# Gated delta-rule attention with mixture of experts on one core: block inverse by joining, decay exponents from spread rows, third value tap on VectorE

## Chip, cores and metric

One core of a Trainium2 chip. The metric is the device time of one launch in microseconds. Everything is fp32.

## What is computed

The reference, cut to the part that matters here (b=2 sequences, t=2048 tokens, 16 heads of 64; a mixture of 64 experts follows in the same launch and is not touched by the change):

```python
q, k, v = (causal_dwconv(x @ W.T, w, bias) for ...)      # 4 taps per channel
g = log_sigmoid(x @ Wg.T); beta = sigmoid(x @ Wb.T)
k = k / clip(norm(k), 1e-12); q = q * Kd ** -0.5
def step(S, inp):                                        # over time, per head
    Sk = einsum('bhkv,bhk->bhv', S, k_t)
    delta = einsum('bhv,bhk->bhkv', v_t, k_t) - einsum('bhv,bhk->bhkv', Sk, k_t)
    S = exp(g_t) * S + b_t * delta
    o_t = einsum('bhkv,bhk->bhv', S, q_t)
x = layernorm(x + o @ Wo.T)
x = layernorm(x + moe(x))
```

## The kernel before, in words

A first phase (`gates_phase`, some 54 us) computes the gates. Their running sums lie with 64 positions on the partitions in `za`; transposed by TensorE they are stored in DRAM as `g_rows`.

The second phase (`delta_phase`, L190) is a software pipeline over 64 macros. A macro `m` is 256 tokens of both sequences for one pair of heads; a chunk is 64 tokens. Slot `t` works on macro `t` (projections, first taps), `t-1` (other taps, gates, masked products), `t-5` (assembling the inverse of a 64x64 triangular matrix per chunk from its 16x16 diagonal blocks) and, from `t-7` on, on the sequential chain over chunks (two chain steps per slot, called one and two). Two macros are a group; the inverses of the 16x16 diagonal blocks are made for a whole group at once, spread over an odd slot and the even slot behind it. Each engine has its own instruction order written out by hand in a loop over the slots (TensorE L534, VectorE L669, ScalarE L811, GpSimd L906, SyncE's DMA queue L345), and semaphores tie them together. What the change touches:

- The convolution has four taps. ScalarE makes tap 3 (`last_tap`, L731) and copies the projection to `hist` (L729); VectorE adds taps 2, 1, 0 for k and q in place (`conv`, L575, line 586). For v it adds taps 2 and 1 (`conv_values`, L589, line 599), and tap 0 is a second product with a diagonal matrix, accumulated in PSUM while TensorE transposes the values (`turn_values`, L403, line 416). The diagonal lies in the last 64 columns of the weight buffer.
- The decay exponents of a macro (key's running sum subtracted from query's, minus infinity above the diagonal) are one product of two operands `arg_l` and `arg_r` (`exponents`, L421), into the single PSUM bank `p_j` that the three projections use too. One ScalarE instruction takes their exponential into `ex` (`decay`, L739, line 744), GpSimd multiplies by beta over the squared key length (`weight`, L886, line 890), VectorE multiplies the products by it (`mask`, L622, line 628).
- The diagonal blocks: 128 partitions hold one 16x16 block each. GpSimd sets `xi` to the identity (L922); `substitute` (L631) then takes 15 rows, each an outer product into `outer` (line 639) and a subtraction from `xi` (line 642), every instruction waiting for the one before it. Row `r` has (15-r)(r+1) elements: 15, 28, 39, 48, 55, 60, 63, 64 and down again. Rows 0 to 7 stand in the odd slot, rows 8 to 14 in the even one.
- `horner` (line 649) subtracts a product in PSUM from the loaded inverse three times per macro, with a product of TensorE between each two (`inverse_ry1`, `inverse_ry2`, line 448). In TensorE's order the third projection, `inverse_ry1`, `products` (L432, line 439) and `inverse_ry2` end a slot. `mask` waits for `products`.
- `lengths` (line 616) sums the squared keys, GpSimd's `clip` (line 877) bounds them, VectorE takes the reciprocal (`inverse_lengths`, line 620), GpSimd makes two factors (883, 884), `weight`, and the square root (`roots`, L893, line 896), by which ScalarE scales the values one slot later (line 792).
- GpSimd also decays the state before each chain step (`decay_state`, line 902), takes out the off-diagonal part (`off_diagonal`, line 872), and copies three columns of history (858, 865).

## Time and profile before

| | us |
|---|---|
| median of 3 runs | 1730.0 (1725.58 to 1736.51) |
| the profiled execution | 1728.8 |
| its span, first to last instruction | 1727.0 |
| busy in the span: TensorE | 1546.2 (90%) |
| VectorE | 1238.0 (72%) |
| ScalarE | 888.3 (51%) |
| GpSimd | 852.2 (49%) |

The span holds three stages: gates up to about 54 us, the delta phase to about 1177 us, the mixer and experts to the end. The shares are means over all of them, so each stage has to be read by itself. PE and PEld are TensorE's products and its weight loads, DVE is VectorE, ACT ScalarE, POOL GpSimd, SP SyncE. A line number L is that of the kernel before. On VectorE, records of neighbours overlap by some 80 ns where the second waits for nothing.

### The profile page before, as it was taken

The numbers are of one execution on the slowest core, as the hardware profiler recorded it, in microseconds if no ns is written. First come the engines' busy times: TensorE is split into PE (matmuls) and PEld (weight loads), VectorE is DVE, ScalarE is ACT, GpSimd is POOL, SyncE is SP. The second block draws the span as 40 slices with busy tenths as digits, with TensorE's granted clock in tenths as the row PEclk, the third lists the DMA queues.
The fourth block names the chain that finished last, engine by engine and source line by source line (L and its number), as shares of the span: only waits on it lengthen the run. The fifth ranks groups of instructions, "written<-read, shape, count | busy, mean of one in ns | idle before, by whom it ended". The sixth has DMA issues, their size and how long they took to land. (4 is left out here: it accounts for less than half of the span.)

```text
span 1727.0 us, 73955 instructions
## 1 busy us (share of the span) xinstructions
PE 1546.2 (90%) x31244; PEld 1160.5 (67%) x31244; DVE 1238.0 (72%) x3061; ACT 888.3 (51%) x2282; POOL 852.2 (49%) x1070
## 2 busy tenths in 40 slices
PE   6678999999999999999999999778899998898980
PEld 6235666666666666666666666666899998887870
DVE  1488999999999999999999999633566665222225
ACT  1466767777777677677777676510111111332333
POOL 0034354344444444435435444312777777677775
PEclk9899999999999999999999999989999999999995
DMA  8345555656556655655665655536565631799658
GB/s 320 87 88 116 126 117 130 133 110 134 129 116 132 126 122 119 141 122 116 128 137 117 126 120 117 114 74 191 175 185 164 186 98 41 208 249 248 135 86 301
DMA packets 521402, 245.45 MB, mean 142 GB/s; under 512 B 423888, under 2 KB 485968, under 8 KB 520176
## 3 DMA queue, kind: packets, MB, share of 16 engines
q1 hardware_dynamic: 367824, 200.45, 44.1%
q10 hardware_dynamic: 134784, 21.25, 7.7%
q0 software_dynamic: 18464, 19.03, 6.3%
q8 instruction: 247, 4.05, 1.0%
q14 instruction: 83, 0.68, 0.1%
HBM read 169.29 MB, written 71.37 MB: 139 GB/s over the span
## 5 line engine op out<-in xcount | busy, mean ns | idle before, releaser
L387 PE MATMUL delta_p_j<-xt,w 128*128 128x512 f32 x768 | 386.1, 626 | 20.6 <-ACT delta_yv L736 8.3
L586 DVE SCALAR_TENSOR_TENSOR delta_kq<-delta_hist,cw,delta_kq 128x512 f32<-128x512 f32 x384 | 315.5, 822 | 22.9 <-ACT delta_kq L736 13.9
L729 ACT ACTIVATE delta_hist<-delta_p_j 128x512 f32<-128x512 f32 x192 | 115.0, 599 | 256.3 <-PE delta_p_j L387 244.3
L902 POOL TENSOR_TENSOR delta_sd<-state,eg_end 128x256 f32<-128x256 f32 x128 | 92.2, 720 | 290.6 <-DVE state L665 290.6
L387 PEld LDWEIGHTS delta_p_j<-xt,w 128*128 128x128 f32 x768 | 131.5, 191 | 135.8 <-issue 101.9
L1406 POOL DMA_INDIRECT slot_tokens<-tokens,mix_slot x192 | 189.3, 986 | 64.0 <-issue 52.2
L877 POOL TENSOR_SCALAR delta_n<-delta_n 128x8 f32<-128x8 f32 x64 | 15.5, 242 | 318.9 <-DVE delta_n L616 318.9
L1176 PE MATMUL mix_p_h<-wo,w 128*88 128x128 f32 x1024 | 127.9, 279 | 13.2 <-ACT wo L1362 12.6
L1176 PEld LDWEIGHTS mix_p_h<-wo,w 128*88 128x88 f32 x1024 | 117.1, 159 | 30.6 <-ACT wo L1362 28.5
L1312 DVE SCALAR_TENSOR_TENSOR wo<-wo,mix_p_h 88x256 f32<-88x256 f32 x64 | 26.7, 417 | 154.7 <-ACT wo L1368 154.7
L792 ACT ACTIVATE delta_kpv<-delta_kpv,delta_root 128x64 f32<-128x64 f32 x512 | 135.6, 347 | 0.0
L642 DVE TENSOR_TENSOR delta_xi<-delta_xi,delta_outer 128x15 f32<-128x15 f32 (+7 forms) x480 | 122.8, 256 | 16.5
L507 PEld LDWEIGHTS delta_p_c<-delta_r,delta_kkq 64*64 64x64 f32 x2048 | 71.2, 137 | 94.0 <-issue 49.3
L448 PEld LDWEIGHTS delta_p_i<-delta_kkq,rt 64*32 64x32 f32 (+1 forms) x4096 | 67.2, 100 | 92.2 <-DVE delta_kkq L649 68.7
L786 ACT ACTIVATE delta_kpv<-delta_kpv,delta_fk 128x64 f32<-128x64 f32 x512 | 128.8, 341 | 0.0
L599 DVE SCALAR_TENSOR_TENSOR delta_yv<-delta_hist,cw,delta_yv 128x512 f32<-128x512 f32 x128 | 121.6, 950 | 4.8 <-ACT delta_yv L736 4.8
L896 POOL TENSOR_TENSOR delta_root<-delta_n,half_power 128x8 f32<-128x8 f32 x64 | 119.6, 1869 | 0.0
L639 DVE TENSOR_TENSOR delta_outer<-delta_xi,delta_kb 128x15 f32<-128x15 f32 (+7 forms) x480 | 106.2, 221 | 18.6 <-DMA delta_kb<-n_scratch 7.2
L1429 POOL DMA_INDIRECT acc<-mix_ot,mix_places x64 | 100.6, 1573 | 36.1 <-ACT mix_ot L1374 19.1
L448 PE MATMUL delta_p_i<-delta_kkq,rt 64*32 64x32 f32 (+1 forms) x4096 | 81.0, 184 | 31.2 <-DVE delta_kkq L649 31.0
L736 ACT ACTIVATE delta_kq<-delta_p_j,cw 128x512 f32<-128x512 f32 x128 | 99.2, 775 | 0.0
L507 PE MATMUL delta_p_c<-delta_r,delta_kkq 64*64 64x64 f32 x2048 | 89.0, 227 | 5.4 <-DVE delta_r L657 4.9
(155 smaller groups left out, 3579.3 us busy)
## 6 DMA issues: line engine op xcount, KB each, us to landing
delta_xd<-x_scratch SPq DMA_DIRECT2D x256, 128.0 KB, 4.5
w<-in_wqkv SPq DMA_DIRECT2D x64, 416.0 KB, 4.1
w<-in_w SPq DMA_DIRECT2D x64, 352.0 KB
delta_eg<-eg_rows SPq DMA_DIRECT2D x128, 130.0 KB
n_scratch<-delta_kkq ACTq DMA_DIRECT2D x128, 128.0 KB
ot<-o SPq DMA_DIRECT2D x128, 128.0 KB, 3.2
w<-in_w SPq DMA_DIRECT2D x64, 176.0 KB
xt<-ot SPq DMA_DIRECT2D x8, 1024.0 KB, 5.8
```

What stands on the lines that cost most here:

```text
L387: mm = pe.matmul(p_j[:, :], w[e][:, (ch * 3 + n) * 128:(ch * 3 + n) * 128 + 128], xt[m // 8 % 2][:, ch * 512:ch * 512 + 512], start=ch == ...
L448: mm = pe.matmul(view(p_i, g * C + first, (1, count), parts=(64 * sh, rows)), view(lhs, g * C, (1, rows), parts=half(sh)), view(rhs, at + ...
L507: mm = pe.matmul(view(p_c, b * 512 + 128 + q * C, (1, C), parts=half(sh)), view(kkq, ring(group * 2 + q) + b * 256 + c * C, (1, C), parts= ...
L586: ve.scalar_tensor_tensor(out, view(hist[e], i * 2 * 518 + tap, (259, 2), (1, 256)), cw[:, column:column + 1], out, ALU.mult, ALU.add).the ...
L599: ve.scalar_tensor_tensor(out, view(hist[e], 518 + tap, (259, 2), (1, 256)), cw[:, column:column + 1], out, ALU.mult, ALU.add).then_inc(co ...
L642: ve.tensor_tensor(view(xi, row + 1, (SUB, i), (1, left)), view(xi, row + 1, (SUB, i), (1, left)), view(outer, 0, (left, i), (1, left)), A ...
L729: ac.activation(view(hist[e], n * 518 + 3, (259, 2), (1, 256)), p_j[:, :], ACT.Copy)
L786: ac.activation(kpv[:, at:at + C], kpv[:, at:at + C], ACT.Copy, scale=fk[:, g:g + 1]).then_inc(kp_out, 1)
L792: ac.activation(kpv[:, at:at + C], kpv[:, at:at + C], ACT.Copy, scale=root[:, g:g + 1]).then_inc(vp_out, 1)
L896: po.tensor_tensor(root[:, :], n2[:, :], view(s.half_power, 0, (0, 8)), ALU.pow).then_inc(small, 1)
L1176: mm = pe.matmul(p_h[e % 2][0:HALF, piece * 128:piece * 128 + 128], s.w13[:, at * 704 + ch * SI + piece * HALF:at * 704 + ch * SI + piece ...
L1406: po.indirect_dma_start(out=s.tok.ap(), out_offset=bass.IndirectOffsetOnAxis(ap=slot[i % 2][:, k:k + 1], axis=0), in_=tokens[:, i:i + 1], ...
```

## The change

It does four things in the delta phase. (1) The sums of the query are spread over the partitions by DMA into `span`, VectorE adds a constant mask to them (`limit`, one slot ahead), and eight ScalarE exponentials of 64 columns take the key's sum as their bias. (2) The block inverse starts with 1x1 to 4x4 steps on four blocks at once and joins 4x4 to 8x8 and 8x8 to 16x16 by a multiplication of all terms and a sum over them: 15 instructions for 30. (3) Tap 0 of the values goes from TensorE to VectorE. (4) Orders and waits: the taps of k are parted in even slots, tap 2 of the values stands ahead of `horner` in every slot, GpSimd's `roots` goes to the slot after and has two buffers, and GpSimd waits in three places for VectorE. The diff, cut:

```diff
@@ sync
-                    sp.wait_ge(exped, m - 1)
+                    sp.wait_ge(exped, 8 * (m - 1))
                 for sh in range(2):
-                    sp.dma_start(view(arg_l[e], sh * C, (1, C), parts=(64 + sh * 8, 8)), ...
-                sp.dma_start(view(arg_r[e], 0, (1, 512), parts=(80, 2)), ...
+                    sp.dma_start(span[e][64 * sh:64 * sh + 64, :],
+                                 bass.AP(s.g_rows, m * 1024 + sh * 512, [[0, C], [1, 512]])).then_inc(r_in[e], 16)
@@ sync, slot loop
-                    load_rows(t)
                     load_decays(t)
...
                     load_weights(t + 1)
+                if is_macro(t + 1):
+                    load_rows(t + 1)
@@ tensor
-                if n == 1 and m >= 1:
-                    pe.wait_ge(exped, m)
+                if n == 1:
+                    pe.wait_ge(tap_k, m + 1)
...
-                if is_macro(before):
-                    exponents(before)
...
-                    for first in (True, False):
+                    for b, h in QUADS:
+                        mm = pe.matmul(view(p_xy, b * 512 + 256 + c * C, (1, C), parts=half(h ^ b)),
+                                       view(yv[e], b * 256 + c * C, (1, C), parts=half(h)),
+                                       view(const, C_ID + 64 * h, (1, C), parts=half(h)), start=True, stop=True)
@@ vector
+            def limit(m):
+                ve.wait_ge(r_in[e], 32 * (m // 2 + 1))
+                ve.tensor_tensor(view(span[e], 0, (C, 8), (1, C)), view(span[e], 0, (C, 8), (1, C)),
+                                 view(const, C_LATER, (0, 8), (1, C)), ALU.add).then_inc(limited, 1)
+            def begin_blocks(group):
+                ve.tensor_tensor(xi[:, :], const[:, C_EYE:C_EYE + SUB * SUB], kb[:, :], ALU.subtract)
+                for row in (1, 2):
...
+                    ve.tensor_tensor(view(joint, 0, (2, 4), (left, row), (1, left)), ..., ALU.mult)
+                    ve.tensor_tensor(view(xi, row + 1, blocks, (SUB, row), (1, left)), ..., ALU.add)
+            def joined(size, left, left_row, right, count):
+                for k in range(2 if size == 4 else 1):
+                    ve.tensor_tensor(view(terms, k * 64, (size * size, size), (size, size), (1, size)),
+                                     view(left, k * (16 if left_row == size else 136), (left_row, size), (0, size), (1, size)),
+                                     view(xi, right + k * 136, (0, size), (1, size), (SUB, size)), ALU.mult)
+            def join_fours(group):
+                joined(4, xi, SUB, 4, at)
+                ve.tensor_reduce(joint[:, 0:32], view(terms, 0, (4, 32), (1, 4)), AX.X, ALU.add)
+                joined(4, joint, 4, 4 * SUB + 4, at + 3)
+                ve.tensor_reduce(view(xi, 4, (136, 2), (SUB, 4), (1, 4)), ...)
+            def join_eights(group, part):
+                joined(8, ...)
+                ve.tensor_reduce(out, view(terms, 0, (64, 8), (8, 8), (1, 8)), AX.X, ALU.add)
@@ vector, slot loop
                     conv_values(before, 1)
+                    conv_values(before, 0)
                     conv(before, 1, tap_q, conv_q)
                     gate(before)
...
                 if even:
-                    substitute(subst_group, range(8, 11))
+                    join_eights(small_group, 0)
...
                 if even:
-                    substitute(subst_group, range(11, SUB - 1))
-                if is_macro(m) and t % 2 == 0:
-                    conv(m, 0, tap_k, conv_k)
-                if odd:
-                    substitute(subst_group, range(0, 2))
+                    join_eights(small_group, 1)
                 if is_macro(before):
                     lengths(before)
                 if odd:
-                    substitute(subst_group, range(2, 4))
+                    begin_blocks(small_group)
+                if is_macro(m) and t % 2 == 0:
+                    conv(m, 0, tap_k, conv_k, (2,))
                 if is_macro(before):
                     inverse_lengths(before)
+                if odd:
+                    join_fours(small_group)
+                if is_macro(m) and t % 2 == 0:
+                    conv(m, 0, tap_k, conv_k, (1,))
+                if is_macro(t + 1):
+                    limit(t + 1)
                 if is_macro(mi):
                     horner(mi, rx_done, 16, y1_out)
-                if odd:
-                    substitute(subst_group, range(4, 8))
+                if is_macro(m) and t % 2 == 0:
+                    conv(m, 0, tap_k, conv_k, (0,))
                 if two_:
                     update(*two_)
-                if is_macro(m) and t % 2 == 0:
+                if is_macro(m):
                     conv_values(m, 2)
                 if is_macro(mi):
                     horner(mi, ry1_done, 32, y2_out)
-                if is_macro(m) and t % 2:
-                    conv_values(m, 2)
                 if is_macro(before):
                     mask(before)
@@ scalar
+                for g in units:
+                    ac.activation(view(ex[e], g * (C + 1) + 1, (1, C)), span[e][:, g * C:g * C + C], ACT.Exp,
+                                  bias=s.minus_cum[:, m * 8 + g:m * 8 + g + 1]).then_inc(exped, 1)
... (even macros: all eight in slot m behind last_tap of v; odd macros: four in slot m, four in slot m + 1)
@@ gpsimd, slot loop
+                if is_macro(before):
+                    po.wait_ge(conv_v, 3 * before + 1)
                 if one:
                     decay_state(*one)
...
-                    po.tensor_copy(xi[:, :], const[:, C_EYE:C_EYE + SUB * SUB]).then_inc(xi_set, 1)
+                if is_macro(before):
+                    po.wait_ge(conv_q, 3 * before + 3)
+                if is_macro(t - 2):
+                    roots(t - 2)
                 if two_:
+                    po.wait_ge(r_out, two_[0] * 4 + two_[1] + 1)
                     decay_state(*two_)
                 if is_macro(before):
                     clip(before)
                     factors(before)
                     weight(before)
-                    roots(before)
```

The start loads no `arg_l` and `arg_r` (four DMAs less), the weight buffer loses its 64 columns of diagonals, and the gates phase adds one ScalarE copy of 512 columns (`minus_cum`).

## Rows read from the trace of the kernel before

**Rows 1.** Busy time of each engine, 500 to 900 us: us, busy (instructions), clock, DMA

```profile
500.00:900.00 400.00, 386.23 (x10461) 260.84 (x10454) 373.53 (x824) 286.15 (x731) 175.25 (x255) 1.00 0.60 125
```

**Rows 2.** Who waited for whom, 500 to 700 us: in total, times, longest

```profile
PEld delta_p_i L448 <- DVE delta_kkq L649: 12.6, 17, 1.9
...
DVE delta_kkq L649 <- PE delta_p_i L448: 0.3, 1, 0.3
```

**Rows 3.** The mask's line, whole run: duration ns min/median/max, first and last start

```profile
L628 DVE TENSOR_TENSOR delta_kkq<-delta_p_xy,ex x64: 1210/1217/1225, 79.3 to 1106.9; 128x1024 f32<-128x1024 f32 x64
```

**Rows 4.** VectorE in order of time, two slots: start, us, operation

```profile
600.70 2.32 DVE L586 SCALAR_TENSOR_TENSOR delta_kq<-delta_hist,cw,delta_kq 128x512 f32<-128x512 f32 x3
...
611.80 0.20 DVE L620 RECIPROCAL delta_rn<-delta_n 128x8 f32<-128x8 f32 x1 [0.36 <-POOL delta_n L877]
...
612.67 1.36 DVE L599 SCALAR_TENSOR_TENSOR delta_yv<-delta_hist,cw,delta_yv 128x512 f32<-128x512 f32 x1
...
614.28 1.22 DVE L628 TENSOR_TENSOR delta_kkq<-delta_p_xy,ex 128x1024 f32<-128x1024 f32 x1
...
616.61 3.07 DVE L586 SCALAR_TENSOR_TENSOR delta_kq<-delta_hist,cw,delta_kq 128x512 f32<-128x512 f32 x3
...
624.16 0.17 DVE L639 TENSOR_TENSOR delta_outer<-delta_xi,delta_kb 128x15 f32<-128x15 f32 x1
624.36 0.18 DVE L642 TENSOR_TENSOR delta_xi<-delta_xi,delta_outer 128x15 f32<-128x15 f32 x1
```

**Rows 5.** GpSimd in order of time, the same stretch

```profile
612.43 1.04 POOL L890 TENSOR_TENSOR ex<-ex,delta_bp 128x512 f32<-128x512 f32 x1
...
616.10 1.44 POOL L872 TENSOR_TENSOR noff<-delta_kkq,const 128x384 f32<-128x384 f32 x1
617.49 0.66 POOL L858 COPY delta_hist<-carry 128x18 f32<-128x18 f32 x1
```

**Rows 6.** VectorE by line and shape, 200 to 1020 us: busy us, mean ns, idle before

```profile
L586 DVE SCALAR_TENSOR_TENSOR delta_kq<-delta_hist,cw,delta_kq 128x512 f32<-128x512 f32 x300 | 248.4, 828 | 7.1
L599 DVE SCALAR_TENSOR_TENSOR delta_yv<-delta_hist,cw,delta_yv 128x512 f32<-128x512 f32 x100 | 96.6, 966 | 0.0
L609 DVE TENSOR_TENSOR delta_kqg<-delta_kq,delta_eg 128x1024 f32<-128x1024 f32 x50 | 61.3, 1225 | 10.4 <-DVE delta_kq L586 9.4 <-PE delta_p_c L519 1.0
...
L616 DVE TENSOR_REDUCE delta_n<-delta_sq 128x8 f32<-128x512 f32 x49 | 33.3, 679 | 0.0
...
L642 DVE TENSOR_TENSOR delta_xi<-delta_xi,delta_outer 128x63 f32<-128x63 f32 x50 | 21.0, 420 | 1.7
...
L642 DVE TENSOR_TENSOR delta_xi<-delta_xi,delta_outer 128x55 f32<-128x55 f32 x49 | 18.8, 384 | 1.7
L639 DVE TENSOR_TENSOR delta_outer<-delta_xi,delta_kb 128x55 f32<-128x55 f32 x49 | 17.4, 354 | 0.9
```

**Rows 7.** The 15-element multiply: row 14 (608.2 us), then row 0 (624.2 us)

```profile
L639 DVE TENSOR_TENSOR delta_outer<-delta_xi,delta_kb 128x15 f32<-128x15 f32 x1 | 0.2, 177 | 0.0
...
L639 DVE TENSOR_TENSOR delta_outer<-delta_xi,delta_kb 128x15 f32<-128x15 f32 x1 | 0.2, 168 | 0.0
```

**Rows 8.** TensorE in order of time, the same stretch

```profile
602.86 1.36 PE L429 MATMUL delta_p_j<-arg_r,arg_l 82*128 82x512 f32 x2
...
612.48 0.70 PE L448 MATMUL delta_p_i<-delta_kkq,rt 64*32 64x32 f32 x32 [0.40 <-DVE delta_kkq L649]
613.10 1.10 PE L439 MATMUL delta_p_xy<-delta_kq 64*64 64x128 f32 x32
```

**Rows 9.** ScalarE by line and shape, 500 to 700 us

```profile
L786 ACT ACTIVATE delta_kpv<-delta_kpv,delta_fk 128x64 f32<-128x64 f32 x100 | 25.2, 341 | 0.0
...
L744 ACT ACTIVATE ex<-delta_p_j 128x512 f32<-128x512 f32 x12 | 7.2, 598 | 5.1 <-PE delta_p_j L429 5.1
```

**Rows 10.** SyncE's queue in order of time, an odd slot

```profile
622.94 0.54 SPq L290 DMA_DIRECT2D w<-in_wqkv  x1
```

**Rows 11.** DMA issues of the page: count, KB each, us to landing

```profile
w<-in_wqkv SPq DMA_DIRECT2D x64, 416.0 KB, 4.1
```

More of the change, by code:

```diff
@@ L242, in delta_phase @@
         SLOTS = NM + 7
+        STEPS = 15
         def ring(m):
@@ L574, in _, with conv @@
         def _(ve):
-            def conv(m, i, tapped, done):
+            def conv(m, i, tapped, done, taps=(2, 1, 0)):
                 e = m % 2
                 out = view(kq[e], i * 512, (256, 2), (1, 256))
-                for tap in (2, 1, 0):
+                for tap in taps:
                     if tap == 2:
@@ new lines, in join_fours @@
+            def join_fours(group):
+                at = group * STEPS + 5
+                joined(4, xi, SUB, 4, at)
+                ve.wait_ge(inverted, at + 2)
+                ve.tensor_reduce(joint[:, 0:32], view(terms, 0, (4, 32), (1, 4)), AX.X, ALU.add).then_inc(inverted, 1)
+                joined(4, joint, 4, 4 * SUB + 4, at + 3)
+                ve.wait_ge(inverted, at + 5)
+                ve.tensor_reduce(view(xi, 4, (136, 2), (SUB, 4), (1, 4)), view(terms, 0, (64, 2), (16, 4), (4, 4), (1, 4)),
+                                 AX.X, ALU.add).then_inc(inverted, 1)
@@ new lines, in join_eights @@
+            def join_eights(group, part):
+                at = group * STEPS + 11 + 2 * part
+                if part == 0:
+                    joined(8, xi, SUB, 8, at)
+                    out = joint[:, :]
+                else:
+                    joined(8, joint, 8, 8 * SUB + 8, at)
+                    out = view(xi, 8, (SUB, 8), (1, 8))
+                ve.wait_ge(inverted, at + 1)
+                ve.tensor_reduce(out, view(terms, 0, (64, 8), (8, 8), (1, 8)), AX.X, ALU.add).then_inc(inverted, 1)
@@ L667, in update @@
                                  view(p_c, 256, (512, 2), (C, 2), (1, C)), ALU.add).then_inc(s_out, 1)
+            limit(0)
             for t in range(SLOTS):
@@ L671, in _ @@
                 one, two_ = chain_step(t, 0), chain_step(t, 1)
-                subst_group = (t - 3) // 2
-                odd, even = t % 2 == 1 and 0 <= subst_group < NG, t % 2 == 0 and 0 <= subst_group < NG
+                small_group = (t - 3) // 2
+                odd, even = t % 2 == 1 and 0 <= small_group < NG, t % 2 == 0 and 0 <= small_group < NG
                 if is_macro(mi - 1):
@@ L821, in _ @@
                     last_tap(m, 0, kq[m % 2][:, 0:512], tap_k)
-                if is_macro(t - 2):
-                    scale_values(t - 2, range(0, 4))
-                if is_macro(before):
-                    decay(before)
+                if is_macro(t - 3):
+                    scale_values(t - 3, range(4, 8))
+                if is_macro(before) and t % 2 == 0:
+                    decay(before, range(4, 8))
+                if is_macro(m) and t % 2:
+                    decay(m, range(0, 4))
                 if is_macro(before):
@@ L830, in _ @@
                 if is_macro(t - 2):
-                    scale_values(t - 2, range(4, 8))
+                    scale_values(t - 2, range(0, 4))
                 if is_macro(m):
@@ L837, in _ @@
                     last_tap(m, 2, yv[m % 2][:, :], tap_v)
+                if is_macro(m) and t % 2 == 0:
+                    decay(m, range(0, 8))
                 if t % 2 == 0 and 0 <= (t - 4) // 2 < NG:
@@ L1516, in constants @@
     c[:, C_REST:C_REST + 128] = i >= j
+    c[:, C_LATER:C_LATER + C] = np.where(i[:, :C] % C <= j[:, :C], 0, NEG)
     return c
-def exponent_operands():
-    import numpy as np
-    left, right = np.zeros((128, 128), np.float32), np.zeros((128, 512), np.float32)
-    key, query = np.indices((C, C))
-    for n in range(8):
-        right[0:C, n * C:n * C + C] = np.where(key <= query, 0, NEG)
-        for sh in range(2):
-            right[64 + sh * 8 + n, n * C:n * C + C] = -1
-    for sh in range(2):
-        left[0:C, sh * C:sh * C + C] = np.eye(C)
-        left[80 + sh, sh * C:sh * C + C] = 1
-    return left, right
 def kernel(**inputs):
```

128 lines of the change are left out of this document (49 added, 79 removed).

## The prediction

> **What bounds the kernel now.** I read the page's table of 40 slices first: two thirds of the span, the delta phase, have TensorE and VectorE both near full. So the averages of the page (VectorE 72%) say nothing of it, and I cut the phase out by a view of busy time in stretches. From 500 to 900 us TensorE is busy 386 of 400 us and VectorE 373.5, at a granted clock of 1.00 [rows 1]. Two engines this full cannot both be the bound, so the next view is who waited for whom: in 200 us TensorE's weight loads waited 12.6 us for the `horner` results of VectorE, and VectorE waited 0.3 us for the products that feed them [rows 2]. TensorE waits for VectorE, and hardly the other way. VectorE's 26 us without a record in those 400 us are 824 instructions at some 35 ns. **VectorE sets the slot.** The mask comes 64 times from 79.3 to 1106.9 us, so a slot is 16.3 us [rows 3], and I count VectorE's time per pair of slots, since the block inverse takes two.
>
> The second thing to see is that VectorE is slowed. A tap in three dependent ones takes 0.77 us (2.32 for three), the same three take 3.07 from 616.61 on; a single one from 612.67 takes 1.36 [rows 4]. Beside them GpSimd works: `weight` from 612.43 to 613.47, `off_diagonal` from 616.10 to 617.54, and then GpSimd's own copy of 18 columns takes 0.66 us [rows 5]. The mask, which reads PSUM, is 1210 to 1225 ns always [rows 3]. So instructions with two operands in SBUF and GpSimd's hold each other up, those with one in PSUM don't. The sum of that, over 50 slots: taps of q and k (828 - 742) ns x 300 = 25.8 us, taps of v (966 - 742) x 100 = 22.4, and in `substitute` (420 - 224) x 50 + (384 - 217) x 49 + (354 - 209) x 49 = 25.1 [rows 6]; 742, 224, 217 and 209 are these groups' undisturbed durations. Together 73.3 us, 2.9 us per pair.
>
> **The change part by part, VectorE, per pair of slots.** A dependent instruction starts 35 ns behind the end of the one before (624.16 + 0.17, next at 624.36 [rows 4]), an independent one some 80 ns before it. A multiply of two SBUF operands takes 168 ns for 15 elements and 1225 for 1024 [rows 6, 7]: 1.04 ns per element and 0.15 us.
>
> - `substitute` goes: 30 instructions whose undisturbed durations by that line add to 6.2 us, plus 25 dependent gaps less five overlaps: 6.6 us removed.
> - The joins come: one of 256 elements (0.45 with its gap), four small ones (0.8), in `join_fours` four of 64 and two sums of 128 (1.4), in `join_eights` two of 512 (0.72) and two sums (0.68 by the row of `lengths` [rows 6], 0.6 where the next is independent), 2.7, less overlaps: 5.1 us. But one operand of each join is read down a column, 16 elements apart. The only such reading in the trace on VectorE is row 14 of `substitute`: 177 ns where row 0, the same 15 elements in line, takes 168 [rows 7]; 0.6 ns an element. On 2 x 512 + 4 x 64 elements that is 0.8 us. Bounds: nothing, and double (the difference is 9 ns). I take 5.9. Net -0.7.
> - Tap 0 of v: two dependent steps of 0.78 = +1.57.
> - `limit`: two of 512 elements, 0.69 less the overlap = +1.22.
> - The taps of k parted in even slots lose two dependent gaps: -0.24.
> - In even slots the reciprocal waits 0.36 us for `clip` today [rows 4]. A tap now stands between; but it has two SBUF operands and begins before `clip` can, so `clip` waits it out as the copy of 18 columns did [rows 5], and the reciprocal still waits some 0.3. -0.12 in all.
> - Meetings with GpSimd. `decay_state` of step one now starts behind tap 2 of v and runs, with `off_diagonal` behind it, beside `horner`, mask, `horner` and `residual`, 2.0 us of PSUM readers: those meetings go (about 1.0 us per pair), that of `decay_state` with `conv` and `substitute` goes too (it starts beside a join already running, or beside the sum of `lengths`), and the copy to `xi`. `weight` stays: in even slots it falls, with the two factors ahead of it, on `limit` and tap 0 (0.86), in odd ones on `join_fours` (0.85). 2.9 becomes 1.7: -1.2. Bounds: one meeting left (0.85), or all of the old 2.9.
> - A new wait. In odd slots `substitute` rows 4 to 7 stood between `horner` and mask. Now `update`, tap 2 and `horner` follow the first `horner` and are through 1.24 us after its end. The mask needs `products`, which stand behind `inverse_ry1` on TensorE: started at 612.48 upon that result, ended at 614.20, 1.8 us after it [rows 8]. So VectorE waits 0.55 us in odd slots. In even ones tap 0 of k fills the gap. Behind the mask are queued `horner` and `residual`, thus the chain. Bounds: nothing, 0.6.
>
> Sum: -0.7 + 1.57 + 1.22 - 0.24 - 0.12 - 1.2 + 0.55 = +1.1 us per pair. On 31 pairs: +33 us.
>
> The rule of the Trainium skill that speaks most against this change is in "Vector Engine (DVE) Microarchitecture Reference", the paragraph on the SBUF access granule: a port keeps its rate only on runs of two or more adjacent words, and one source that hops every element takes 1.73 ns a column in place of 1.05. By that figure the estimate for the columns is 0.87 us per pair in place of 0.8, and the sum 2 us more; by a flat rate it would be 25 us less.
>
> **Other engines.** TensorE loses `exponents`, 1.36 us at 602.86 with the wait inside it [rows 8], and half of `turn_values`, some 0.5 us: 1.6 to 1.9 us a slot. It was not the bound, so in full slots it only waits longer for VectorE. In the first three or four slots, before inverse and chain begin, the single bank `p_j` passes from projection to ScalarE and back and VectorE idles: there I give back 1.6 x 3, -5 us. ScalarE pays 0.25 us for each of eight exponentials (25.2 us for 100 [rows 9]) for one of 0.60: +1.4 a slot. Most fall in even slots, which by my count reach 16.9 us of ScalarE's work; it spills up to 1 us into the odd slot, where it has 4 us to spare. Cost nothing; were that cover gone, TensorE's next projection would wait up to 1 us per pair. DMA: two loads of 128 KB for three small ones, behind the weights in SyncE's queue. In odd slots those are issued at 622.94 [rows 10] and take a median of 4.1 us [rows 11]. The rows would land near 628 to 630, and `limit` stands near 629. I take zero, bounds zero to 1.0 us per pair. The start loads four operands fewer, ahead of a wait for other things: nothing.
>
> Total: 33 - 5 = +28 us. Against the profiled execution's 1728.8 (span 1727.0) this is 1757; the median of the runs shown is 1.2 higher, 1730.0, so I say 1758.
>
> **Rivals.** First, the meetings with GpSimd all go. The three new waits on GpSimd place each of its instructions beside PSUM readers or sums; if `weight` too costs nothing, 1.7 us per pair fall out: 1.1 - 1.7 = -0.6, 31 pairs -18, and -5: 1707. For it: this is the largest waste in the trace, and the waits fit it. Against it: `weight` still follows the reciprocal at once, beside instructions of two SBUF operands in both slots. The result turns to faster from about 0.8 us of meetings left per pair, one where I count two. Chance 0.18. Second, a draw: reading columns costs nothing (-0.8) and the mask's wait is hidden by the meeting ahead of it (-0.3): 0.0 per pair, 1725 to 1735. For it: 9 ns are thin evidence. Against it: the order of the mask is written down. Chance 0.25. Third, the rows come late: the wait of `limit` in odd slots, 0.5 to 1 us more per pair, moves `horner`, TensorE and mask with it: +15 to +31, 1773 to 1789. For it: a transfer queued behind 416 KB and block loads. Against it: the weights' wait for `turned` ends earlier. Chance 0.15. Fourth, TensorE were the bound after all: then up to 1.6 us a slot came back, toward 1690; rows 2 speak plainly against it, and it holds 0.02 inside the first rival's 0.18.
>
> **Numbers.** My forecast has 0.42, the rest as given. A per cent, 17 us, is about what a measurement of this kernel can tell from no change. Faster by more: 0.18. Within: 0.25 and a little of the forecast's lower part, 0.27. Slower: 0.55. The range from 1707 (first rival) to 1792 (third) leaves out 2 in 10; the forecast's own is 1745 to 1772.
>
> **What would show it.** Right: a mean slot of 16.8 us by the mask's line; VectorE without idle time except for TensorE ahead of the mask in odd slots, about 0.5 us; joins of 512 elements at 1.0 us; a tap or `limit` or small join stretched by `weight` in each slot, and no tap stretched by `off_diagonal`; TensorE idle about 2 us a slot. Wrong: joins of 512 at 0.7 us, taps all at 0.74 us, a VectorE that waits for rows or for ScalarE, or slots under 16.3 us.

## The result

| | before | after |
|---|---|---|
| median, us | 1730.7 (4 runs, 1725.58 to 1736.51) | 1785.9 (4 runs, 1771.39 to 1793.17) |
| profiled execution, us | 1728.8 | 1771.4 |
| its span, us | 1727.0 | 1769.6 |

The ratio of the mean times is 1.031, with a 95% interval from 1.0235 to 1.038: slower, by 55 us between the medians where the prediction had 28. The profiled execution is the quickest of its four, so the trace has only 42.6 us of the 55 to show. Its mean granted clock is 0.953; those of the other three are 0.951, 0.942 and 0.939, and the slowest has the lowest. What the last 12 us or so are stands in no trace.

### The profile page after: what moved, and what is told of

It reads as the page before. It is cut to its first block and busy times, and to the rows that moved or that the text cites. A ratio compares the mean times of both kernels' runs of the same rounds, so it can differ in the third digit from the quotient of the medians.

```text
span 1769.6 us, 69722 instructions
## 1 busy us (share of the span) xinstructions
PE 1473.1 (83%) x29068; PEld 1122.9 (63%) x29068; DVE 1272.5 (72%) x2709; ACT 962.9 (54%) x2731; POOL 828.1 (47%) x1038
## 5 line engine op out<-in xcount | busy, mean ns | idle before, releaser
L384 PE MATMUL delta_p_j<-xt,w 128*128 128x512 f32 x768 | 399.4, 644 | 27.8 <-ACT delta_yv L760 14.0
L564 DVE SCALAR_TENSOR_TENSOR delta_kq<-delta_hist,cw,delta_kq 128x512 f32<-128x512 f32 x384 | 300.0, 781 | 7.9 <-ACT delta_kq L760 1.0
L933 POOL TENSOR_TENSOR delta_sd<-state,eg_end 128x256 f32<-128x256 f32 x128 | 101.2, 790 | 341.4 <-DVE delta_r L677 174.7
L927 POOL TENSOR_TENSOR delta_root<-delta_n,half_power 128x8 f32<-128x8 f32 x64 | 106.5, 1664 | 271.5 <-DVE delta_kq L564 271.5
L384 PEld LDWEIGHTS delta_p_j<-xt,w 128*128 128x128 f32 x768 | 135.5, 196 | 147.6 <-issue 106.8
L577 DVE SCALAR_TENSOR_TENSOR delta_yv<-delta_hist,cw,delta_yv 128x512 f32<-128x512 f32 x192 | 144.9, 755 | 4.1 <-ACT delta_yv L760 1.8
L1207 PE MATMUL mix_p_h<-wo,w 128*88 128x128 f32 x1024 | 128.6, 280 | 13.4 <-ACT wo L1393 12.5
L769 ACT ACTIVATE ex<-delta_span,minus_cum 128x64 f32<-128x64 f32 x512 | 131.9, 342 | 0.0
L428 PE MATMUL delta_p_i<-delta_xd,noff 64*64 64x48 f32 x2048 | 75.5, 223 | 34.2 <-DMA delta_xd<-x_scratch 28.4
L462 PE MATMUL delta_p_c<-state,delta_kqg 64*64 64x64 f32 x2048 | 63.3, 237 | 44.7 <-DVE state L685 44.1
L612 DVE TENSOR_TENSOR delta_kkq<-delta_p_xy,ex 128x1024 f32<-128x1024 f32 x64 | 78.0, 1219 | 25.0 <-PE delta_p_xy L419 24.9
```

Source lines behind the costliest of these rows:

```text
L384: mm = pe.matmul(p_j[:, :], w[e][:, (ch * 3 + n) * 128:(ch * 3 + n) * 128 + 128], xt[m // 8 % 2][:, ch * 512:ch * 512 + 512], start=ch == ...
L428: mm = pe.matmul(view(p_i, g * C + first, (1, count), parts=(64 * sh, rows)), view(lhs, g * C, (1, rows), parts=half(sh)), view(rhs, at + ...
L564: ve.scalar_tensor_tensor(out, view(hist[e], i * 2 * 518 + tap, (259, 2), (1, 256)), cw[:, column:column + 1], out, ALU.mult, ALU.add).the ...
L577: ve.scalar_tensor_tensor(out, view(hist[e], 518 + tap, (259, 2), (1, 256)), cw[:, column:column + 1], out, ALU.mult, ALU.add).then_inc(co ...
L769: ac.activation(view(ex[e], g * (C + 1) + 1, (1, C)), span[e][:, g * C:g * C + C], ACT.Exp, bias=s.minus_cum[:, m * 8 + g:m * 8 + g + 1]). ...
L927: po.tensor_tensor(root[m % 2][:, :], n2[:, :], view(s.half_power, 0, (0, 8)), ALU.pow).then_inc(small, 1)
```

## The profile after

Where the time went is told by the mask, as in [rows 3]: its line over the whole run (durations in ns, first and last start), then the eight of the first 208 us, then all that begin from 200 to 1020 us.

```profile
L612 DVE TENSOR_TENSOR delta_kkq<-delta_p_xy,ex x64: 1210/1224/1225, 77.6 to 1153.5; 128x1024 f32<-128x1024 f32 x64
...
L612 DVE TENSOR_TENSOR delta_kkq<-delta_p_xy,ex x8: 1215/1225/1225, 77.6 to 190.5; 128x1024 f32<-128x1024 f32 x8
...
L612 DVE TENSOR_TENSOR delta_kkq<-delta_p_xy,ex x47: 1210/1224/1225, 208.6 to 1004.2; 128x1024 f32<-128x1024 f32 x47
```

The same view of the kernel before has its ninth mask at 202.8 us, and 50 of them up to 1010.1. So the first mask comes 1.7 us earlier than before, the ninth 5.8 later (208.6 against 202.8), the last 46.6 later, and what follows the last is 4.0 us shorter. The mean slot is 17.08 us (1153.5 - 77.6 over 63). In the full part a pair of slots takes 2 x (1004.2 - 208.6) / 46 = 34.59 us, where it took 2 x (1010.1 - 202.8) / 49 = 32.95: **1.64 us more, predicted 1.1.**

Busy time from 500 to 900 us, columns as in [rows 1]:

```profile
500.00:900.00 400.00, 335.00 (x9074) 232.16 (x9072) 361.52 (x655) 296.04 (x846) 155.79 (x228) 0.98 0.60 132
```

VectorE fell from 373.5 to 361.5 us. Per pair of slots it is busy 31.26 us (361.52 x 34.59 / 400) against 30.77 before, 0.49 more, and without a record 3.33 us against 2.18, 1.15 more. So the larger part of the loss is no work but waiting. For what, the waits say (VectorE's own, 200 to 1020 us: us in total, times, longest):

```profile
DVE delta_span L593 <- DMA delta_span<-g_rows: 22.2, 20, 2.3
DVE delta_kkq L612 <- PE delta_p_xy L419: 16.0, 24, 1.5
DVE delta_kqg L587 <- DVE delta_kq L564: 10.2, 47, 0.6
DVE delta_kkq L669 <- PE delta_p_i L428: 2.9, 4, 1.5
```

and the same of before:

```profile
DVE delta_kqg L609 <- DVE delta_kq L586: 9.4, 45, 0.6
DVE delta_rn L620 <- POOL delta_n L877: 9.1, 25, 0.4
DVE delta_kkq L649 <- PE delta_p_i L448: 4.8, 11, 1.0
...
DVE delta_kkq L628 <- PE delta_p_xy L439: 0.9, 2, 0.6
```

Over 24 pairs of slots the wait of `limit` for its rows is 0.93 us a pair, a new one; the mask's wait for `products` is 0.67, up from 0.04. The reciprocal's wait for `clip` (9.1 us) has gone. The two new waits belong together, as one odd slot of VectorE shows (start, us, operation, in brackets the idle time before it):

```profile
614.21 1.30 DVE L638 TENSOR_TENSOR rows<-delta_joint,delta_xi 128x64 f32<-128x64 f32 x2
615.54 0.29 DVE L650 TENSOR_REDUCE delta_xi<-rows 128x32 f32<-128x128 f32 x1
618.09 0.69 DVE L593 TENSOR_TENSOR delta_span<-delta_span,const 128x512 f32<-128x512 f32 x1 [2.27 <-DMA delta_span<-g_rows]
618.70 0.55 DVE L669 TENSOR_TENSOR delta_kkq<-delta_xd,delta_p_i 128x384 f32<-128x384 f32 x1
...
622.35 1.23 DVE L612 TENSOR_TENSOR delta_kkq<-delta_p_xy,ex 128x1024 f32<-128x1024 f32 x1 [1.51 <-PE delta_p_xy L419]
```

TensorE in the same slot:

```profile
613.54 1.98 PE L384 MATMUL delta_p_j<-xt,w 128*128 128x512 f32 x4
619.30 1.07 PE L428 MATMUL delta_p_i<-delta_kkq,rt 64*32 64x32 f32 x32 [3.78 <-DVE delta_kkq L669]
620.30 1.98 PE L419 MATMUL delta_p_xy<-delta_kq 64*64 64x128 f32 x32
```

and SyncE's queue:

```profile
608.12 0.38 SPq L298 DMA_DIRECT2D delta_kb<-n_scratch  x1
608.55 3.28 SPq L278 DMA_DIRECT2D delta_eg<-eg_rows  x2
611.92 0.53 SPq L287 DMA_DIRECT2D w<-in_wqkv  x1
612.50 1.10 SPq L270 DMA_DIRECT2D delta_span<-g_rows  x2
```

The rows are the last of four loads: issued at 612.50, there at 618.09, 5.6 us later. `limit` could have begun at 615.82. `horner` is queued behind it, and `inverse_ry1` on TensorE waits for `horner`: TensorE stands still for 3.78 us. Then its two groups take 1.07 and 1.98 us, where before they took 0.70 and 1.10 [rows 8], and the mask waits 1.51 instead of the 0.55 that I had forecast. The granted clock of this stretch says why:

```profile
610.00:615.00 5.00, 5.00 (x88) 3.00 (x86) 4.39 (x14) 2.81 (x9) 2.08 (x5) 1.00 0.59 138
615.00:625.00 10.00, 6.22 (x134) 4.23 (x132) 5.97 (x13) 3.17 (x10) 2.05 (x5) 0.83 0.72 166
```

It is 1.00 up to 615 and 0.83 on average in the 10 us with the wait. Cut finer, it is 1.00 up to 619 and then

```profile
620.00:622.00 2.00, 2.00 (x46) 1.81 (x42) 0.66 (x2) 0.00 (x0) 1.68 (x4) 0.50 0.84 255
```

so `products` ran at the lower level of 1.2 GHz, behind an engine that had been idle for 3.78 us up to 619.30, and the clock is back at 1.00 from 623 on. Slots with a short wait for rows keep the short mask wait: in the odd slot at 580 us, `limit` waits 0.20 us and the mask 0.63.

Last, VectorE's instructions by line and shape, 500 to 900 us (busy us, mean ns, idle before):

```profile
L577 DVE SCALAR_TENSOR_TENSOR delta_yv<-delta_hist,cw,delta_yv 128x512 f32<-128x512 f32 x67 | 50.0, 746 | 0.8
...
L593 DVE TENSOR_TENSOR delta_span<-delta_span,const 128x512 f32<-128x512 f32 x23 | 15.9, 691 | 12.3 <-DMA delta_span<-g_rows 12.3
...
L638 DVE TENSOR_TENSOR rows<-delta_joint,delta_xi 128x64 f32<-128x64 f32 x24 | 12.5, 559 | 0.4
L638 DVE TENSOR_TENSOR rows<-delta_xi 128x512 f32<-128x512 f32 x11 | 11.4, 1035 | 0.0
L638 DVE TENSOR_TENSOR rows<-delta_joint,delta_xi 128x512 f32<-128x512 f32 x11 | 11.2, 1020 | 0.0
...
L638 DVE TENSOR_TENSOR rows<-delta_xi 128x64 f32<-128x64 f32 x24 | 5.7, 281 | 0.0
L604 DVE RECIPROCAL delta_rn<-delta_n 128x8 f32<-128x8 f32 x23 | 4.6, 199 | 1.5
```

Taps of v take 746 ns where they took 966 (742 undisturbed), so hardly anything stretches them any more. The second pair of small joins takes 559 ns where its twin takes 281: `weight` runs beside it. Joins of 512 take 1.03 us.

## The experiments

Three accounts stood against each other. The **late rows** (theory 1): the load is too late for `limit`, and the wait is paid in full. The **DMA itself** (theory 2): either its place in SyncE's queue (2a), or its bytes, 256 KB a slot, which hold up the loads beside it (2b). The **clock** (theory 3): TensorE idles more and is therefore slow when it is needed. Beside these stand the terms of my own sum. Ratios are to the kernel before on the same chip, with their 95% interval; 1 point is 1% of the time, 17 us. To set beside them, the change as a whole is at 1.031; its own interval is 0.7 points to either side, so what is taken from it is known to about 13 us at best.

**Rows at the head of the queue.** The load of the rows moves from the end of a slot's loads to their head.

```diff
+                if is_macro(t + 1):
+                    load_rows(t + 1)
                 if t % 2 and 0 <= (t - 3) // 2 < NG:
                     load_blocks((t - 3) // 2)
                 if is_macro(t):
                     load_decays(t)
...
-                if is_macro(t + 1):
-                    load_rows(t + 1)
```

> The changed kernel (median 1786 us) with the loads of the spread rows at the head of SyncE's slot, ahead of block, decay and weight loads. Theory 1 (VectorE's own order sets the slot; in odd slots limit waits 1.07 us per pair for rows queued behind the weights): VectorE's waits for rows go, about 31 pairs x 1.0 = 30 us less, 1755 us. Rival (the rows' wait only fills time in which VectorE would wait for TensorE at a lower granted clock): 1775 us or more, the wait reappears ahead of the mask.

Measured: 1.033 [1.030, 1.036], 1783 us: nothing gained. VectorE's waits, 200 to 1020 us:

```profile
DVE delta_kkq L669 <- PE delta_p_i L428: 17.2, 16, 1.5
DVE delta_kkq L612 <- PE delta_p_xy L419: 14.0, 24, 0.6
DVE delta_r L677 <- PE delta_p_c L462: 14.0, 12, 2.1
DVE delta_xi L624 <- DMA delta_kb<-n_scratch: 13.4, 13, 1.8
```

The wait for rows (22.2 us) is gone from the list, and 13.4 us for the diagonal blocks have come, whose load now stands behind the rows, with 17.2 and 14.0 for products of TensorE. TensorE waits 53.1 us for the load of the finished inverses (`delta_xd`), 18.1 in the change as it is. The wait has moved and has not gone. The load also has to wait for the exponentials that still read its buffer, and at the head of the queue it holds up everything behind it: SyncE waits 257.7 us for them, 26.3 in the change as it is. The mask's longest wait is back at 0.6 us.

**`limit` behind `horner`.** In odd slots the first `horner` goes ahead of `limit`, so that TensorE has its input before VectorE waits for rows.

```diff
-                if is_macro(t + 1):
+                if is_macro(t + 1) and t % 2 == 0:
                     limit(t + 1)
                 if is_macro(mi):
                     horner(mi, rx_done, 16, y1_out)
+                if is_macro(t + 1) and t % 2:
+                    limit(t + 1)
```

> The changed kernel with limit placed behind the first horner in odd slots, in the gap that VectorE waits for inverse_ry1 and products. Theory 1: the wait ahead of horner and mask (0.75 us per pair) is filled and the rows have 0.55 us more to come: 1.1 to 1.3 us per pair less, about 37 us, 1749 us. Rival (these waits are the lower clock of TensorE, whose products get longer the longer it idles): the wait keeps its length behind limit, 1770 us or more.

Measured: 1.016 [1.013, 1.020], 1750 us. The way is that of theory 1, the size is not: 1.4 points less, 25 us (give or take 14), where 37 were expected. That 1750 us look like the expected 1749 is the chip's doing, on which the kernel before takes 1723.5 us and not 1730.7. In its waits the rows still cost 15.9 us, the mask only 3.2 (16.0 after the change). So by the waits more was won of what followed from the rows (12.8 us ahead of the mask) than of the wait for them (6.3).

**The rows from GpSimd's queue,** `limit` as in the last one. The load leaves SyncE's queue altogether.

```diff
@@ gpsimd, slot loop, behind the copies of history
+                if is_macro(t + 1):
+                    load_rows(t + 1)
@@ sync, slot loop
-                if is_macro(t + 1):
-                    load_rows(t + 1)
```

> a2 (limit behind horner in odd slots) with the rows loaded from GpSimd's queue, right behind its history copies, in place of SyncE's. Theory 2a (SyncE's queue is what is late: 256 KB behind weights and blocks, and behind each other): the wait of limit goes without another one coming up, 0.6 us per pair less than a2, ratio 1.00 to 1.005. Theory 2b (the engines of the DMA are shared, and the bytes themselves are what is late): waits move to blocks and inverses as in a1, ratio 1.016 or more.

Measured: 1.058 [1.0545, 1.061], 1827 us, the worst of all. It lies on the side of 2b, but it doesn't speak for it. GpSimd in order of time:

```profile
610.06 0.19 POOL L894 COPY carry<-delta_hist 128x18 f32<-128x18 f32 x1
617.55 1.14 POOL L934 DMA_DIRECT2D delta_span<-g_rows  x2 [7.31 <-ACT ex L768]
618.71 1.68 POOL L926 TENSOR_TENSOR delta_root<-delta_n,half_power 128x8 f32<-128x8 f32 x1
620.37 0.61 POOL L941 TENSOR_TENSOR delta_sd<-state,eg_end 128x256 f32<-128x256 f32 x1
```

GpSimd waits 7.31 us for ScalarE's exponentials before it may issue, and the decay of the state, which the chain needs, is queued behind. The largest new wait of the run is another: TensorE waits 67.5 us (23 times, up to 4.0) for the load of the finished inverses, 18.1 in the change and 22.4 with `limit` behind `horner` alone. What makes that load so late no run shows, so the 4 points above that run are explained only in part. The bytes are the same in all three, so this run tested my placement, not the bytes; for these see the rows that nobody reads, below.

**Part 1 undone.** The exponents go back to a product of TensorE and one ScalarE exponential; no `limit`, no spread rows. Parts 2, 3 and 4 stay.

```diff
+                if is_macro(before):
+                    exponents(before)
...
-                if is_macro(t + 1):
-                    limit(t + 1)
...
-                if is_macro(m) and t % 2 == 0:
-                    decay(m, range(0, 8))
```

> The changed kernel with its first part undone: the exponents are TensorE's product again with one exponential, loaded by three small DMAs, no limit and no spread rows. Theory 2 (the loads of the spread rows, 256 KB a slot, are late and make others late, and limit adds 0.61 us a slot): VectorE per pair is before's 32.9 - 0.7 (joins) + 1.57 (tap 0) - 0.24 - 1.8 (meetings) + 0.55 (mask) = 32.3 us, so about 20 us under the kernel before: ratio 0.99, 1705 to 1715 us. Rival (TensorE takes back its 1.1 to 1.4 us a slot and becomes the bound, or the joins are what costs): ratio 1.01 or more.

Measured: 0.986 [0.984, 0.989], 1706 us, as expected. Without part 1 the change is 1.4% quicker than before; part 1 alone costs 1.031 less 0.986, 4.5 points or 77 us, give or take 13. Where it costs them the mask's line tells:

```profile
L623 DVE TENSOR_TENSOR delta_kkq<-delta_p_xy,ex x51: 1208/1214/1225, 212.6 to 1018.6; 128x1024 f32<-128x1024 f32 x51
```

A pair of slots takes 2 x (1018.6 - 212.6) / 50 = 32.24 us, 2.35 less than with part 1 (34.59). And from the first mask to the ninth it is 117.3 us (79.25 to 196.53), where it is 131.0 with part 1 and 123.5 before.

**Parts 1 and 3 undone.** Tap 0 of v returns to TensorE as well. What stays is the joining and the orders and waits.

```diff
-                    conv_values(before, 0)
...
-                    for b, h in QUADS:
+                    for first in (True, False):
```

> First and third part undone: the kernel before with joins for substitutions and the new orders and waits of VectorE and GpSimd alone. VectorE per pair 30.7 us by theory 1. TensorE's work of a slot is that of before, 16.0 us by its timeline, 32.0 a pair. Theory: TensorE is the bound now, 32.1 us a pair, ratio 0.985, about 1700 us. Rival (VectorE's sum alone counts): 30.7 a pair, ratio 0.96, 1660 us.

Measured: 0.982 [0.979, 0.985], 1696 us, as expected. The busy time from 500 to 900 us and the first of VectorE's waits from 200 to 1020:

```profile
500.00:900.00 400.00, 392.74 (x10746) 267.35 (x10746) 363.53 (x663) 294.08 (x747) 164.56 (x250) 1.00 0.60 130
```

```profile
DVE delta_kkq L629 <- PE delta_p_xy L440: 24.2, 49, 1.7
DVE delta_kkq L686 <- PE delta_p_i L449: 13.1, 20, 1.0
```

TensorE is busy 393 of 400 us and VectorE waits for it in nearly every slot: the bound has changed sides. Joins and orders relieve VectorE so far that TensorE sets the slot. How much of it is the joins and how much the orders no run parts.

**Rows that nobody reads.** To the kernel without part 1 the two row loads of every slot are added, into a spare buffer (the 256 KB of part 1, at its place in the queue). Their numbers are not used.

```diff
+                if is_macro(t + 1):
+                    if t >= 1:
+                        sp.wait_ge(spare_in, 32 * t)
+                    for sh in range(2):
+                        sp.dma_start(s.erows[64 * sh:64 * sh + 64, 0:512],
+                                     bass.AP(s.g_rows, (t + 1) * 1024 + sh * 512, [[0, C], [1, 512]])).then_inc(spare_in, 16)
```

> c1 (first part undone, ratio 0.986) plus the two loads of spread rows a slot, 256 KB, at the place behind the weights where the change has them, into a buffer that nobody reads. Theory 2b (the bytes make other loads late): waits for blocks and inverses come up that c1 lacks, 15 us or more, ratio 0.995 to 1.01. Rival (only the instruction that waits for the rows is late, others don't feel them): ratio 0.986 to 0.989.

Measured: 0.986 [0.982, 0.990], 1702 us, the same as without the loads. The stretch from 500 to 900 us moves 142 GB/s in place of 126, and from 200 to 1020 us the waits for loads grow by 0.7 us on VectorE and 1.2 on TensorE. The bytes cost nothing that could be told (0.1 points less, give or take 0.5), and theory 2b, which wanted 15 us or more, falls. One thing of part 1 this run leaves out: its loads don't wait for the exponentials, and in the changed kernel that wait (26.3 us of SyncE's queue) stands ahead of the loads of the inverses.

**An addition that nobody reads.** To the kernel without part 1 one addition of 512 elements a slot is added where `limit` stands. Its result is not used, and it waits for no load.

```diff
+                if is_macro(t + 1):
+                    limit(t + 1)
                 if is_macro(mi):
                     horner(mi, rx_done, 16, y1_out)
```

> c1 plus one addition of 512 columns a slot at limit's place, on a buffer that nobody reads, with no load behind it. Theory 1: 0.61 us a slot on VectorE, 64 slots, 39 us: ratio 1.009. Rival (VectorE has slack by now, since c1 leaves TensorE near full): under 20 us, ratio 0.997 or less. What d1 and d2 leave of the first part's 78 us (1.031 or 1.033 less 0.986) is the wait of limit for its rows and what that moves.

Measured: 1.005 [1.003, 1.006], 1732 us, a little under what was expected: 1.0047 less 0.9863 is 1.8 points, 32 us. It is 0.51 us a slot for an instruction of 0.69 us that steps 0.61. So 32 of part 1's 77 us are simply one more instruction on the full engine, and bytes are none of them. Some 45 us are left, give or take 13.

**`inverse_rx` twice.** In the changed kernel TensorE makes its products for the first `horner` a second time with the same operands, to keep it busy: some 33 products a slot more by the counts of the trace (9846 for 9074 from 500 to 900 us).

```diff
+                by_unit(rt, xd[m % 2], 0, 16, 48, d_extra)
                 by_unit(rt, xd[m % 2], 0, 16, 48, rx_done)
```

> The changed kernel with the 16 products of inverse_rx issued twice in a row (same result): TensorE has 0.9 us more work a slot, in its slack. Theory 3 (part of the loss is TensorE's granted clock, 0.98 in the phase in place of 1.00, which falls after long idle time and then stretches the products ahead of the mask): clock back to 0.99 or more in the phase, wait ahead of the mask from 0.75 to 0.5 us per pair, 1765 to 1780 us, less than the changed kernel. Rival (the clock plays no part): 1786 us or some more, since horner gets its product later.

Measured: 1.0335 [1.031, 1.036], 1785 us. The granted clock from 500 to 900 us is 0.99 in place of 0.98, over the whole run 0.959 in place of 0.953, and the mask's wait 13.6 us in place of 16.0; the time is the same, where theory 3 had 1765 to 1780 us. So little moved that it settles nothing: a clock held at full could be worth no more here than the extra products cost. For theory 3 as the size of the miss it is no support.

**Tap 0 back to TensorE,** in the changed kernel, part 1 kept.

```diff
-                    conv_values(before, 0)
...
-                    for b, h in QUADS:
+                    for first in (True, False):
```

> The changed kernel with tap 0 of the values back on TensorE as a second product with the diagonal (the third part undone). Theory 1: two steps of 0.78 us leave VectorE per pair, 31 x 1.57 = 49 us less, 1737 us, and TensorE, 0.5 us a slot fuller, idles less. Rival (TensorE is now the bound, or ScalarE, fuller by eight exponentials): no gain or a loss, 1786 us or more.

Measured: 1.027 [1.024, 1.030], 1771 us: 0.4 points under the change, inside the two intervals, where theory 1 had 49 us. VectorE's waits:

```profile
DVE delta_span L599 <- DMA delta_span<-g_rows: 43.7, 25, 3.3
DVE delta_kkq L618 <- PE delta_p_xy L425: 20.4, 26, 1.5
```

VectorE has 1.5 us a pair less to do, but the rows are there no earlier: in odd slots `limit` begins 15.3 us behind the mask before it in the median, and in the change 14.8. The wait for them doubles from 22.2 to 43.7 us, 0.9 us a pair more. This shows best what bounded the changed kernel in its odd slots: no longer VectorE's work, but the arrival of the rows.

**Joins along rows.** The second operand of each join is read along a row and no longer down a column. Other numbers of `xi` are multiplied so, and the products are no longer those of the inverse; the count and size of the instructions are the same.

```diff
-                                     view(xi, right + k * 136, (0, size), (1, size), (SUB, size)), ALU.mult)
+                                     view(xi, right + k * 136, (0, size), (SUB, size), (1, size)), ALU.mult)
```

> The changed kernel with the second operand of each join read along rows in place of down columns, elements and counts the same; so the blocks that it inverts are not the inverses. Theory 1 with the price of row 14 of the old substitution (0.6 ns an element hopped): joins of 512 elements fall from 1.03 to 0.69 us, small ones from 0.28 to 0.23, 0.85 us per pair, 26 us less, 1760 us. Rival (columns cost nothing, a join of all terms is slow for another reason, such as its broadcast operand): joins stay at 1.03 us, 1786 us.

Measured: 1.018 [1.014, 1.021], 1756 us: 1.3 points or 23 us (give or take 14) where 26 were expected. By line and shape, 500 to 900 us:

```profile
L638 DVE TENSOR_TENSOR rows<-delta_joint,delta_xi 128x64 f32<-128x64 f32 x24 | 12.6, 563 | 0.4
L638 DVE TENSOR_TENSOR rows<-delta_xi 128x512 f32<-128x512 f32 x12 | 8.2, 684 | 0.0
L638 DVE TENSOR_TENSOR rows<-delta_joint,delta_xi 128x512 f32<-128x512 f32 x12 | 8.2, 684 | 0.0
L638 DVE TENSOR_TENSOR rows<-delta_xi 128x64 f32<-128x64 f32 x24 | 4.3, 221 | 0.0
```

1035 and 1020 ns become 684, 281 become 221: 0.35 + 0.34 + 2 x 0.06 = 0.81 us per pair, where I had 0.8 from a difference of 9 ns. It is 0.69 and 0.66 ns an element in the joins of 512 and 0.9 in those of 64; the pair beside `weight` (559 and 563 ns) gains nothing. The Trainium skill, "Vector Engine (DVE) Microarchitecture Reference", the paragraph on the SBUF access granule, has 1.73 against 1.05 ns a column when one source hops 4 KiB at every element, 0.68 more. The prediction left the 4 KiB out. The hop here is of 16 elements, 64 bytes, and the same paragraph says that small steps cost more than large ones; on 512 elements the runs show the price of the large hop and no more.

**Better versions.** Both start from the kernel without part 1. In the first, `join_fours` goes behind the first `horner`, so that it covers the mask's wait:

```diff
-                if odd:
-                    join_fours(small_group)
                 if is_macro(m) and t % 2 == 0:
                     conv(m, 0, tap_k, conv_k, (1,))
                 if is_macro(mi):
                     horner(mi, rx_done, 16, y1_out)
+                if odd:
+                    join_fours(small_group)
```

> c1 with join_fours behind the first horner in odd slots, in the gap in which VectorE waits 0.55 us for products. Theory 1: that wait goes, 0.5 us per pair, 15 us: ratio 0.977. Rival (TensorE is near its own bound of 15.5 us a slot and cannot deliver earlier): under 5 us, ratio 0.984 or more.

Measured: 0.982 [0.979, 0.986], 1693 us, short of what was expected. The mask's wait falls from 13.7 to 2.7 us in the traces (0.4 us a pair), and the time by 0.4 points, no more than the two intervals leave open. In the second, VectorE makes tap 0 of v for half of the tokens only, and TensorE the other half:

```diff
+                count = 256 if tap else 128
...
-                    for b, h in QUADS:
+                    for first in ((True, False) if c >= 2 else (True,)):
+                        for b, h in QUADS:
```

> d3 with tap 0 of the values on VectorE for half of the tokens and on TensorE for the other half. VectorE loses 0.27 us of each 0.78, TensorE gains 0.25 us a slot. If the two engines are balanced between c1 (VectorE bound) and c2 (TensorE bound, 0.982): 0.5 us per pair under d3, ratio 0.970; if TensorE is the bound already: no better than d3.

Measured: 0.981 [0.976, 0.985], 1689 us. It is the lowest of all and beats both kernels, but can't be told from the last one nor from the one without parts 1 and 3.

```profile
500.00:900.00 400.00, 391.26 (x10386) 262.70 (x10378) 374.99 (x696) 294.82 (x753) 165.59 (x253) 1.00 0.60 131
```

TensorE is busy 391 and VectorE 375 of 400 us, where they were 384 and 383 in the last run: what the one lost the other took over, and the time hardly moved. That is the second of the two cases expected, TensorE near its own bound.

## Why the prediction was half right

The sign and the range held (slower, 1786 us in 1707 to 1792); the forecast's own range, up to 1772, did not. The mechanism for the sign, more work on an engine that is full, was right. The size was off by 28 us. That it stayed inside the range was in part luck: the meetings and the reciprocal below came out 0.88 us a pair too dear in the sum, and on 31 pairs these 27 us hid as much of what was missing. With them right the forecast would have been 1731 us, and the error 55. By its own steps:

- **VectorE bounds, TensorE's relief is worth nothing.** Held: the addition that nobody reads costs 32 us for one instruction a slot. TensorE fell from 386 to 335 us busy, and the time rose.
- **Joins, column reading, tap 0, `limit`.** Held: 1.03 us for 1.0, 0.81 for 0.8 (but from the large joins, and not from all four small ones), 746 ns for 742, 691 for 690. Part 3 costs 0.4 points, 0.986 less 0.982, less than its 1.57 us a pair, because without it TensorE is the bound.
- **The mask's new wait of 0.55 us.** Held where the rows are in time (0.63 at 584.86); the mean of 0.67 has the slots with a slow TensorE in it.
- **Meetings with GpSimd, 2.9 to 1.7 us.** Right in kind, wrong in size: from 200 to 1020 us, 24 pairs, the small joins beside `weight` are busy 24.7 us and their twins without it 11.5, and the taps of q and k take (786 - 742) ns x 282 = 12.4 us too much: 25.6 us, 1.07 per pair. So each of the two meetings cost some 0.5 us where I had 0.85. My first rival had 0.6 of its 1.7 us.
- **The reciprocal still waits 0.3 us.** Wrong, by 0.25 us: 1.5 us idle before 23 of them are 0.07 each. The tap in between did cover `clip`.
- **"DMA: I take zero, bounds zero to 1.0 us per pair."** This is the step that failed: the term was mis-sized, and it measured 0.93 us a pair in the wait alone, and up to 1 us more where TensorE slowed behind it. Both positions were judged well. Counted from the start of the last mask (614.28 in [rows 4]), I had `limit` at 14.7 us and the rows at 13.7 to 15.7. In the odd slot shown above, `limit` could begin at 14.4 (615.82 - 601.39) and the rows came at 16.7; in the one at 580 us it was 13.9 (580.48 - 566.61) and 14.1. Over the 24 odd slots from 200 to 1020 us `limit` begins 13.7 to 16.7 us behind the mask, 14.8 in the median. The fault was to call two times that lie within a microsecond of each other a cost of zero. A wait is never negative: where the rows are early nothing is given back, where they are late all of it is paid. The third rival had the place, the mechanism and the price (1773 to 1789), and I gave it 0.15.
- **The start, -5 us.** Failed too: between the first mask and the ninth the change loses 7.5 us. The first mask came 1.7 us earlier, and that was all. It is part 1 that loses here, 13.7 us against the kernel without it; with the unread addition in that kernel 5.8 us of them are there (77.15 to 200.24 us), and with `limit` behind `horner` 7.9 are given back (74.79 to 197.85). Of VectorE's waits from 60 to 200 us, 4.5 us are for rows, and the granted clock from 100 to 200 us is 0.88 where it was 0.97.
- **ScalarE, "cost nothing".** Not shown in time, for no run takes the eight exponentials alone; but the traces speak against it. They stand ahead of the copy of the finished inverse, in even slots: the inverse's last write ends at 633.20, and the copy begins at 635.72, behind 2.01 us of exponentials. In the kernel without part 1 it began at 627.64, 0.6 us behind its inverse. The load of the inverses comes after this copy: TensorE waits 18.1 us for it from 200 to 1020 us, and not at all before and without part 1. The rows' own wait for the exponentials in SyncE's queue, ahead of this load, may have a part in it.

```profile
632.51 0.69 DVE L663 TENSOR_REDUCE delta_xi<-rows 128x64 f32<-128x512 f32 x1
```

```profile
633.81 2.01 ACT L769 ACTIVATE ex<-delta_span,minus_cum 128x64 f32<-128x64 f32 x8
635.72 0.64 ACT L797 ACTIVATE delta_xit<-delta_xi 128x256 f32<-128x256 f32 x1
```

The sum, then, of part 1's 77 us (give or take 13): 32 for `limit` as work, nothing for bytes, some 29 for the rows' wait (0.93 us on 31 pairs). That leaves 16, hardly more than the uncertainty, for TensorE's slow stretches, the start and the late copy of the inverse, and which of them holds how much stays open. `limit` behind `horner` gave back 25 us, of the wait and of what follows from it together. The profiled executions say the same of the full part: of 2.35 us a pair, 1.0 comes with the unread addition (33.2 for 32.24) and 0.93 is the wait for rows.

My own sum for the change, mended by what was measured, has 1.1 - 0.63 - 0.25 + 0.93 + 0.12 (the mask's) = 1.27 us per pair, where 1.64 were measured: the last 0.4 or so are in no term of it.

## What to carry over

When a change gives an engine a new input, put the load's landing time against the moment at which that engine will arrive **after** the change, and take the mean of the late ones, not the difference of the means: 0.93 us a pair came from two times within a microsecond of each other, and what is saved ahead of such a wait is waited in it (tap 0 undone: 1.5 us saved a pair, 0.9 of them waited). Ask what is queued behind the waiting instruction: letting `horner` go first gave back 25 us. And of a change in four parts, test each by itself: here three of them together are worth 1.4% and one loses 4.5 points.

## What was new of the hardware

- A wait of 3.8 us on TensorE was followed by products that took 1.98 us in place of 1.10, at a granted clock of 0.50: a late load was paid twice, once on VectorE and once in the products behind it.
- 256 KB more a slot, some 16 GB/s, cost nothing that could be told as long as nobody waited for them (0.986 with and without, to 0.5 points).
- A DMA issue on GpSimd that waits for another engine holds up GpSimd's own work behind it: 7.31 us in one slot.
